# Fetching sixteen of each group's 1024 key and value rows through SyncE in a graph attention kernel

## The reference

```python
N, E, D, H, L, FF = (3125, 100000, 128, 8, 2, 512)
for l in range(L):
    xn = layernorm(x)
    xp = xn + (xn @ Wpos + bpos + deg[:, None] * Wdeg[0] + bdeg)
    q, k, v = (xp @ Wq + bq), (xp @ Wk + bk), (xp @ Wv + bv)      # [n, 8 heads, 16]
    att = einsum('ehd,ehd->eh', q[dst], k[src]) / sqrt(16)       # clipped to +-50
    alpha = softmax of att over the edges of one dst
    aggr = segment_sum(v[src] * alpha, dst)
    x = x + aggr @ Wo + bo
    x = x + gelu(layernorm(x) @ W1 + b1) @ W2 + b2
out = layernorm(x_input + x)
```

## Time and profile before

| | |
|---|---|
| runs | 2277.98 us median of 3 (2273.77 to 2279.02) |
| profiled execution | 2278.56 us; its span 2276.8 us |
| busy in the span | PE 61%, DVE 61%, ACT 34%, POOL 68% |
| chain that ended last | POOL 60%, issue 21%, PE 8%, DVE 6%, DMA 2% |
| of that chain, the gathers of L470 | 60% |
| granted TensorE clock | 0.792 of full speed on average |
| DMA | 322.76 MB, 142 GB/s on average; q0 (GpSimd's) 205.10 MB, q1 115.35 MB |

### The profile page before, as it was taken

How to read it: one execution, slowest core, us unless ns; L and a number is a source line. 1 busy time by engine, 2 the same in 40 slices (tenths; PEclk the granted TensorE clock), 3 DMA queues, 4 the chain that set the end, 5 groups by cost and what they waited for, 6 DMA issues and landing times.

```text
span 2276.8 us, 43094 instructions
## 1 busy us (share of the span) xinstructions
PE 1387.2 (61%) x11435; PEld 1300.2 (57%) x11436; DVE 1400.0 (61%) x2221; ACT 778.1 (34%) x1355; POOL 1545.3 (68%) x1644
## 2 busy tenths in 40 slices
PE   6655565566556666666884545556565665666577
PEld 5545555555556556655764545555555665665567
DVE  8885555656655665666557556556556656656664
ACT  3242223323323333332573222233233333333336
POOL 1577777777777777777117777777777777777731
PEclk9877777777877788888896777777778778888779
DMA  3355545555545545543025554555555455455501
GB/s 85 123 164 161 155 156 160 159 152 160 160 151 160 160 153 158 161 155 114 1 66 169 162 160 154 157 161 155 156 160 159 153 160 160 151 160 160 168 22 29
DMA packets 120614, 322.76 MB, mean 142 GB/s; under 512 B 30847, under 2 KB 43300, under 8 KB 120554
## 3 DMA queue, kind: packets, MB, share of 16 engines
q0 software_dynamic: 75072, 205.10, 29.5%
q1 hardware_dynamic: 44644, 115.35, 16.3%
q10 hardware_dynamic: 838, 1.60, 0.3%
HBM read 313.78 MB, written 8.15 MB: 141 GB/s over the span
## 4 chain that ended last, share of the span: by engine, by line
POOL 60%; issue 21%; PE 8%; DVE 6%; DMA 2%; DVEq 1%; ACT 0%; ACTq 0%; POOLq 0%
POOL kv L470 60%; PE ps L1127 2%; PE ps L1133 2%; DVE q_parts L695 2%; DMA kv<-kv_tab,src_idx 1%; PE ps L1049 1%; PE ps L1080 1%; DVE prod L846 1%; DMA x<-in_x 1%; DVE msg L868 1%; DVEq L316 1%; DVE stats L651 0%; PE ps L1043 0%; PE ps L1119 0%; DVE qkv L754 0%
## 5 line engine op out<-in xcount | busy, mean ns | idle before, releaser
L470 POOL DMA_INDIRECT kv<-kv_tab,src_idx x1564 | 1482.9, 948 | 533.9 <-issue 473.4
L1080 PE MATMUL ps<-msg,hot 128*128 128x136 f32 x3904 | 767.7, 375 | 775.1 <-DVE msg L868 650.7
L1080 PEld LDWEIGHTS ps<-msg,hot 128*128 128x128 f32 x3904 | 712.8, 273 | 813.0 <-issue 813.0
L846 DVE TENSOR_TENSOR prod<-kv,ps 128x1024 f32<-128x1024 f32 x196 | 239.3, 1221 | 637.2 <-DMA kv<-kv_tab,src_idx 635.1
L1066 PE MATMUL ps<-q_parts,hotT 128*128 x5856 | 428.2, 238 | 47.9 <-issue 47.6
L1066 PEld LDWEIGHTS ps<-q_parts,hotT 128*128 x5856 | 410.9, 109 | 65.1 <-issue 51.9
L589 ACT ACTIVATE msg<-att 128x64 f32<-128x64 f32 x196 | 50.2, 256 | 1095.6 <-DVE att L859 1091.7
L827 DVE SCALAR_TENSOR_TENSOR hot<-dst_col,neg_base,ps 128x1024 f32<-128x1024 f32 x244 | 312.0, 1279 | 95.9 <-issue 94.7
L582 ACT ACTIVATE dist<-dst_rows,neg_node 128x1024 bf16<-128x1024 int32 x244 | 280.1, 1148 | 185.2 <-issue 171.5
L585 ACT ACTIVATE hotT<-dist 128x1024 bf16 x244 | 257.8, 1057 | 46.8 <-ACT dist L582 45.5
L849 DVE TENSOR_REDUCE dots<-prod 128x64 f32<-128x1024 f32 x196 | 239.1, 1220 | 6.7
(11 more groups left out here) (160 smaller groups left out, 738.3 us busy)
## 6 DMA issues: line engine op xcount, KB each, us to landing
dst_rows<-in_dst SPq DMA_DIRECT2D x194, 512.0 KB, 3.9
kv<-kv_tab,src_idx POOLq DMA_INDIRECT x1564
kv_tab<-qkv SPq DMA_DIRECT2D x6, 768.0 KB, 3.7
out<-x SPq DMA_DIRECT2D x4, 320.0 KB
kv_tab<-qkv SPq DMA_DIRECT2D x2, 512.0 KB, 3.2
kv_tab<-qkv SPq DMA_DIRECT2D x2, 384.0 KB, 3.3
dst_rows<-in_dst SPq DMA_DIRECT2D x2, 336.0 KB, 3.8
hot<-in_L_gnn_W SPq DMA_DIRECT2D x2, 256.0 KB
```

Source lines behind the costliest of these rows:

```text
L470: pool.indirect_dma_start(kv[:, u, c, :], None, kv_tab[l][:, :], bass.IndirectOffsetOnAxis(ap=src_idx[:, c, at(g)], axis=0)).then_inc(kv_i ...
L846: nc.vector.tensor_tensor(prod[:, :].rearrange("p (c d) -> p c d", d=D), kv[:, u, :, 0:D], qd[u % 2].rearrange("p (c d) -> p c d", d=D), A ...
L1080: last = MM(agg[:, bass.ds(pr % 2, 1), :], hot[:, u % 2, c, :], msg[:, u % 2, c, :], start=(c == 0), stop=(c == GC - 1))
```

## The change

For every group but the last, the last 16 rows of the eighth chunk (partitions 112 to 127) are no longer part of GpSimd's gather, which now has 112 row numbers. SyncE reads each of the 16 row numbers from src_idx into a register and issues a DMA of that one row. These are counted in semaphores of their own, single_in, 16 x 16 for a group, for which DVE waits behind its wait for kv_in. SyncE has the rows of groups 0 to 2 behind its load of dst_rows for group 2, after it has waited for the table and for cols_read; from then on those of group g stand behind its load of dst_rows for group g. For groups from 4 on it waits first for the messages of the group four before, as GpSimd does. What is computed stays the same.

```diff
--- before.py
+++ after.py
@@ -38,6 +38,8 @@
 LAST_CHUNKS = -(-ELAST // P)
 MW = D + H
 SLOTS = 4
+BY_SP = 16
+BY_POOL = P - BY_SP
 ROWS = 3
 TURN = 2 * ROWS
 UN = 5
@@ -270,6 +272,7 @@
         self_exp = sem("self_exp")
         self_msg = sem("self_msg")
         kv_in = [sems(f"kv_in{l}_", SLOTS) for l in range(L)]
+        single_in = [sems(f"single_in{l}_", SLOTS) for l in range(L)]
         dist_done = sems("dist_done")
         hotT_ready = sems("hotT_ready")
         hotT_used = sems("hotT_used")
@@ -358,6 +361,16 @@
 
         @block.sync
         def _(sp):
+
+            def gather_rows(l, g):
+
+                u = g % SLOTS
+                if g >= SLOTS:
+                    sp.wait_ge(msg_done[l], g - SLOTS + 1)
+                for p in range(BY_POOL, P):
+                    row = sp.value_load(src_idx[p:p + 1, GC - 1, g:g + 1], min_val=0, max_val=N - 1)
+                    sp.dma_start(kv[p:p + 1, u, GC - 1, :], kv_tab[l][bass.ds(row, 1), :]).then_inc(single_in[l][u], 16)
+
             sp.dma_start(src_ci[:, 0:ER], src_d[0:P * ER].rearrange("(p c) -> p c", c=ER)).then_inc(src_in, 16)
             sp.wait_ge(pad_clear, 1)
             sp.dma_start(src_ci[0:EREST, ER:ER + 1], src_d[P * ER:E].rearrange("(p c) -> p c", c=1)).then_inc(src_in, 16)
@@ -404,6 +417,13 @@
                         sp.wait_ge(exp_done[l - 1], NG)
                     n = min(GE, E - g * GE)
                     sp.dma_start(dst_rows[:, r, 0:n], dst_d[g * GE:g * GE + n].partition_broadcast(P)).then_inc(rows_in[l][r], 16)
+                    if g == ROWS - 1:
+                        sp.wait_ge(tab_out[l], 16 * NU)
+                        sp.wait_ge(cols_read, 2)
+                        for first in range(ROWS):
+                            gather_rows(l, first)
+                    elif ROWS <= g < NG - 1:
+                        gather_rows(l, g)
             sp.wait_ge(self_msg, L * NU)
             sp.wait_ge(q_rest, L * NU)
             sp.wait_ge(tab_out[L - 1], 16 * NU)
@@ -467,8 +487,9 @@
                     elif l == 0 and g == SLOTS - 1:
                         pool.wait_ge(npair_ready, 1)
                     for c in range(LAST_CHUNKS if g == NG - 1 else GC):
-                        pool.indirect_dma_start(kv[:, u, c, :], None, kv_tab[l][:, :],
-                                                bass.IndirectOffsetOnAxis(ap=src_idx[:, c, at(g)], axis=0)).then_inc(kv_in[l][u], 16)
+                        rows = BY_POOL if c == GC - 1 else P
+                        pool.indirect_dma_start(kv[0:rows, u, c, :], None, kv_tab[l][:, :],
+                                                bass.IndirectOffsetOnAxis(ap=src_idx[0:rows, c, at(g)], axis=0)).then_inc(kv_in[l][u], 16)
 
                 pool.wait_ge(kept_in[l], 16 * KEPT_LOADS)
                 pool.wait_ge(z_done[2 * l], NT)
@@ -842,6 +863,8 @@
                     b, shift = word(d)
                     last_group = isinstance(g, int) and g == NG - 1
                     dve.wait_ge(kv_in[l][u], 16 * (GC * i + (LAST_CHUNKS if last_group else GC)))
+                    if not last_group:
+                        dve.wait_ge(single_in[l][u], 16 * BY_SP * (i + 1))
                     dve.wait_ge(hotT_used[l], b + 2)
                     nc.vector.tensor_tensor(prod[:, :].rearrange("p (c d) -> p c d", d=D), kv[:, u, :, 0:D],
                                             qd[u % 2].rearrange("p (c d) -> p c d", d=D), ALU.mult).then_inc(prod_done[l], 1)
```

## The result

| | before | after |
|---|---|---|
| median | 2276.19 us (2273.77 to 2279.02, 4 runs) | 4318.47 us (4314.35 to 4320.94, 4 runs) |
| span of the profiled execution | 2276.8 us | 4319.2 us |
| granted TensorE clock, mean | 0.792 | 0.656 |

The ratio is 1.897, with a 95% interval of 1.8937 to 1.9003. The forecast was 2907 us, with a range of 2480 to 3550: the direction was right, the size far too small.

What follows compares the result with a forecast made beforehand. GpSimd's gathers bound the kernel at 10.0 us a group; SyncE's rows would take over at 13.3 us. From the profiled 2278.6 us, plus 312.5 for layer 0 and 316.1 for layer 1, came 2907 us, range 2480 to 3550.

Steps and rivals of the forecast that it cites:

- What bounds the kernel, and where the bound goes: Loops over edge groups: GpSimd's gathers set a 10.0 us period; the bound moves to SyncE, at 13.3 us.
- The price of a row: SyncE's queue: load, assertion, address, DMA issue and gaps, 0.80 us a row (0.63 to 1.20), sixteen rows 12.8 us.
- The load, 0.28 us: SyncE's read of a row number into a register, priced from TENSOR_LOAD medians on ACT's, PE's and DVE's queues.
- cross-check: ACT's idle 0.74 us reading one pair-table word, 1.43 reading two: a second word with arithmetic and branch costs 0.69 us.
- the forecast's own slope: Whole kernel: each 0.01 us on the price of a row moves the predicted time by 31 us.
- Rival B: A register load on SyncE costs 0.48 us, so 1.00 us a row and 3527 us in all; chance 0.17.
- high end: Upper estimate for a row on SyncE's queue: 1.20 us, with load 0.31, DMA issue 0.43 and six steps; 4149 us.
- The narrower gather: GpSimd's eighth gather with 112 rows saves 0 to 0.12 us; half taken, 12 us, counting only while GpSimd is bound.
- What waits behind SyncE: DVE's product waits for the rows; dst_rows, ACT and PE work, 7.6 or 11.2 us from issue, stays hidden behind them.
- A, hidden: SyncE stays below 0.595 us a row, GpSimd keeps the pace, and the kernel takes 2267 us; chance 0.05.
- C: SyncE's row price is at its low end, 0.63 to 0.69 us: 2379 to 2565 us; chance 0.13.
- D, late landings: Row DMAs queue behind GpSimd's and land after 6 us, not 2.5: some 4 us a layer; within forecast, no separate chance.

Runs made afterwards that it cites:

- e15: Changed kernel with eight rows by SyncE in place of sixteen (GpSimd's eighth gather has 120): 2372.79 us against 2279.19 for the kernel before, ratio 1.0414.
- e1: Changed kernel without register loads, SyncE fetching sixteen fixed table rows per group, so output values differ: 2276.21 us against 2277.4 for the kernel before, ratio 0.999.
- e3: Changed kernel with all sixteen register loads of a group ahead of its sixteen DMAs: 3490.34 us in one run, 828 less than the changed kernel.
- e2: Changed kernel with value_load lacking min_val and max_val, so no check of bounds: 3447.19 us, 871 less than the changed kernel.

## Why the prediction was wrong

**What bounds the kernel, and where the bound goes: right.** GpSimd before; SyncE after, with SPq 73% of the chain. The two queues' sums decide: eight rows came to 2372.79 us in e15, 2374 expected from the measured price, and sixteen fixed rows without loads (e1) to no loss. Where they turn over with register loads, at seven rows, no undisturbed run shows. The stages outside the loops moved by under 6 us, and the direction was right at 0.95.

**The price of a row: this step failed**, "0.28 + 0.02 + 0.06 + 0.26 + 0.18 = 0.80 us". Measured 1.25. Its terms:

- The load, 0.28 us, was 0.50. It came from queues that read one small tile and issue no DMA between the earlier trace rows. Behind a DMA issue a load takes 0.45 to 0.50 (the first load of a group in e3, and all loads of the changed kernel), and in this change one stands ahead of every load: 0.22 us. The page of the Trainium skill named there ("DMA: Bandwidth & Descriptors", Latency and other measured facts), with its 600 ns, would have been nearer for this use, though no load from SyncE took that as its median.
- The check's arithmetic, 0.15 us with 0.03 before it, was missing. The trace of before had it under the same line as the loads of the earlier trace rows, on ACT's queue, with a median of 152 ns (line L316, kernel before; the low end, 46 ns, is another, ahead of the load):

```profile
L316 ACTq FUSED_REGOPS  x454: 46/152/183, 118.6 to 2161.5; - x152
```

  The forecast took the assertion from that line and left the instruction between, and its cross-check hid it: 0.69 us for "a second word with its arithmetic" was read as agreement with 0.28, not as a price of its own. It was the warning: 0.69 us for a load and its company, without any DMA.
- Address 0.066 us, DMA 0.258 and assertion 0.018 were right; six gaps of 0.25 us in all, where five with 0.18 were forecast: 0.07 us.

The three make 0.44 of the 0.45 us that were missing.

With 1.255 us in place of 0.80, the forecast's own slope of 3104 us per us gives 2907 + 1412 = 4319 us, and 4318.47 was measured. This closeness proves little, as 1.255 was worked out from the period of the same run; by the queue's instructions alone, 1.25 us, it is 4304. The proof is that e2 and e3, which take out the missing instruction and the slow load one at a time, gave back 871 and 828 us. So the mechanism held, and the size of one term of the sum, the price of a row, made the error. Rival B had the slow load (3527 us), with a chance of 0.17; with the load at 0.50 alone it would have been 3590 us, and the missing arithmetic and its gap had to come on top to reach 4318. The price came out above even the high end of 1.20. Of that high end's terms the load, 0.31 us, was a median, though the earlier trace rows had single loads of 0.48 to 0.55, and the arithmetic was missing from it as well.

**The narrower gather: within its bounds, near the low one.** Bounds 0 and 0.12 us, half was taken; 0.02 us was measured on the gather itself (0.93 against 0.95), and the next one gave most of it back (0.96). That it fell inside the bounds is partly luck: the reason given, that fewer partitions can't cost anything, is wrong. Gathers of 116, 120 and 121 rows took longer than those of 128.

**What waits behind SyncE: right for sixteen rows.** DVE's product waited for the single rows for 2460.0 of 2465.0 us, so the late dst_rows were covered, though ACT waited 3283.1 us for them. The cover gets thin with fewer rows (e15), and at the end it is gone: in layer 0 the product of group 97 came 8.65 us after that of group 96, waiting for PE, against 8.23 before. A few us were given back, as hoped, but not there: 5.8 us between the product of group 96 and the next layer or the end, most of it behind group 97, and no run shows why.

**The rivals.** A, hidden, needs 0.595 us a row: refuted by a factor of two; where SyncE's share is hidden, in e1, the time is 0.999 of the kernel before. C is refuted: the shortest row took 1.18 us. D, late landings, is refuted: the product of group 96 in layer 1 starts 1.7 us after the last row's issue begins (4211.06 against 4209.4).

## What to carry to other kernels

Before work is moved to an idle engine, write out every instruction that its queue will run for one item, register arithmetic and checks included, from the place in the trace where the same helper is called, and multiply by the items; an engine that waits 1834.7 us still has only 10 us a group. Ask first what the busy engine gets back: if a few rows off a gather are worth 0.014 us at best, there is nothing to buy, and other widths have to be measured, since fewer rows can also take longer. When register loads and DMAs must stand on one queue, put the loads together, and drop the checks of bounds that the data don't need.

## What the runs showed of the hardware that I had not expected

- A register load from SBUF takes 0.26 to 0.28 us when it reads near the last one, and 0.43 to 0.47 behind a jump from partition 0 to 64 or 112 (on SyncE; on ACT 0 to 112 together with a change of tensor), 0.45 to 0.50 at the median behind a DMA issue. Order alone was worth 828 us in e3.
- GpSimd's gather of 1 KB rows is mostly a fixed price, 0.95 us with 128 rows, 0.93 with 112, 0.85 with 16, but not a steady one: 1.27 us with 116, 0.99 with 120, 1.01 with 121. The three dear counts are the ones that 16 doesn't divide; with six counts in all, that is a lead and not shown.
- The granted TensorE clock fell from 0.78 to 0.64 and 0.63 of full speed in the loops when PE's share of them fell from 583 of 988 us to 631 of 2008: it was given less of its 2.4 GHz level while it waited more. The 5856 matmuls that gather q went from a mean of 238 ns (L1066, before) to 301 ns (L1089, after). That was hidden, as PE stood idle for 2672.4 us ahead of them.
